# Single-precision attention and down products, deeper buffers and other due times in a fused mixture-of-experts and linear-attention kernel

## The reference

```python
x = x + 0.5 * ffn(layernorm(x))            # called A here
x = x + attn(layernorm(x))
x = x + 0.5 * ffn(layernorm(x))            # called B here

# ffn: for each token t
shared = (silu(x @ ws_gate.T) * (x @ ws_up.T)) @ ws_down.T
w, idx = top_k(sigmoid(x @ gate_weight.T), 2);  w = 2.5 * w / w.sum()
y[e]   = (silu(x @ w_gate[e].T) * (x @ w_up[e].T)) @ w_down[e].T
out    = shared + sum over the two chosen e of w_e * y[e]

# attn: xx is x shifted by one token
k, v, r = ((x * mix_i + xx * (1 - mix_i)) @ W_i.T for i in "kvr")
state_t = k_t * v_t + exp(time_decay) * state_(t-1)
o_t     = r_t * (time_first * k_t * v_t + state_t)
out     = (layernorm(o) * ln_g + ln_b) @ Wo.T
```

## Time and profile before

| | us |
|---|---|
| time, median of 3 runs | 1225.51 |
| lowest, highest | 1225.27, 1230.39 |
| the profiled execution's own time | 1227.27 |
| its span, first to last instruction | 1225.1 |
| TensorE busy | 939.6 |
| VectorE busy | 877.5 |
| GpSimd busy | 718.4 |
| ScalarE busy | 491.9 |
| mean granted TensorE clock, share of full speed | 0.921 |

### The profile page before, as it was taken

How to read it: one execution, slowest core, us unless ns; L and a number is a source line. 1 busy time by engine, 2 the same in 40 slices (tenths; PEclk the granted TensorE clock), 3 DMA queues, 4 the chain that set the end, 5 groups by cost and what they waited for, 6 DMA issues and landing times.

```text
span 1225.1 us, 26134 instructions
## 1 busy us (share of the span) xinstructions
PE 939.6 (77%) x8624; PEld 665.5 (54%) x8624; DVE 877.5 (72%) x2582; ACT 491.9 (40%) x880; POOL 718.4 (59%) x684
## 2 busy tenths in 40 slices
PE   1787878896778899879799877986799878766350
PEld 0465565673445657656675465855577544763340
DVE  5975748787978985766799887665798978626332
ACT  5433433643434544524554253432356333431130
POOL 2865666237885745477747884337843877306725
PEclk9988989998898999999899999997989988998695
DMA  9878998436275347899773499778973437775793
GB/s 297 221 157 171 251 196 192 87 92 148 83 154 116 104 106 171 193 184 192 191 161 104 134 205 201 177 190 172 210 158 109 112 108 174 167 171 175 166 256 103
DMA packets 340513, 200.86 MB, mean 164 GB/s; under 512 B 255904, under 2 KB 322592, under 8 KB 340256
## 3 DMA queue, kind: packets, MB, share of 16 engines
q1 hardware_dynamic: 314944, 131.94, 46.4%
q0 software_dynamic: 24576, 67.14, 22.7%
q10 hardware_dynamic: 864, 0.12, 0.1%
HBM read 47.05 MB, written 93.32 MB: 115 GB/s over the span
## 4 chain that ended last, share of the span: by engine, by line
POOL 30%; issue 27%; DVE 11%; PE 10%; DMA 9%; SPq 8%; ACT 3%; POOLq 0%; ACTq 0%; DVEq 0%
POOL y_got L811 11%; POOL xsB L793 7%; SPq L718 5%; POOL xsA L793 5%; DVE acc L1262 2%; DMA y_got<-ysA,y_pos 2%; POOL rstd L767 2%; POOL p_exp L784 2%; DMA ysB<-y_sb 2%; DMA y_got<-ysB,y_pos 2%; SPq L691 2%; DVE stat L1277 1%; PE ps L881 1%; POOL acc L819 1%; PE ps L883 1%
## 5 line engine op out<-in xcount | busy, mean ns | idle before, releaser
L881 PE MATMUL ps<-xq,w_hi 128*128 128x128 f16 x1280 | 236.7, 228 | 82.3 <-DMA xq<-xsB 49.3
L883 PE MATMUL ps<-xq,w_hi 128*128 128x128 f16 x1280 | 236.4, 228 | 0.0
L885 PE MATMUL ps<-xq,w_lo 128*128 128x128 f16 x1280 | 236.1, 228 | 0.0
L1262 DVE SCALAR_TENSOR_TENSOR acc<-y_got,share,acc 128x256 f32<-128x256 f32 x256 | 125.1, 530 | 127.0 <-DMA y_got<-ysB,y_pos 78.0
L905 PE MATMUL ps<-wd_hi,hid_h 128*128 (+1 forms) x576 | 161.1, 280 | 51.9 <-issue 20.4
L881 PEld LDWEIGHTS ps<-xq,w_hi 128*128 x1280 | 131.7, 103 | 96.4 <-DMA xq<-xsB 53.3
L793 POOL DMA_INDIRECT xsB<-rows,pos x128 | 135.1, 1056 | 70.2 <-issue 37.2
L793 POOL DMA_INDIRECT xsA<-rows,pos x128 | 135.8, 1061 | 67.1 <-issue 37.4
L1111 ACT CAST hid_h<-hid 128x512 f16<-128x512 f32 x144 | 89.0, 618 | 211.1 <-DVE hid L1234 196.4
L811 POOL DMA_INDIRECT y_got<-ysB,y_pos x128 | 130.2, 1017 | 62.5 <-issue 38.8
L907 PE MATMUL ps<-wd_hi,hid_l 128*128 (+1 forms) x576 | 161.4, 280 | 0.0
(11 more groups left out here) (157 smaller groups left out, 2148.0 us busy)
## 6 DMA issues: line engine op xcount, KB each, us to landing
ysA<-y_sb SPq DMA_DIRECT2D x40, 512.0 KB, 3.5
ysB<-y_sb SPq DMA_DIRECT2D x40, 512.0 KB, 3.6
acc<-in_x_dram SPq DMA_DIRECT2D x16, 512.0 KB, 4.9
out_dram<-acc SPq DMA_DIRECT2D x16, 512.0 KB
xsA<-zeros SPq DMA_DIRECT2D x36, 128.0 KB
xsB<-zeros SPq DMA_DIRECT2D x36, 128.0 KB
acc<-in_w_chunks_dram SPq DMA_DIRECT2D x10, 384.0 KB, 8.8
xq<-xsA SPq DMA_TRANSPOSE x160
```

The source lines that it names most:

```text
L881: nc.tensor.matmul(half, w_hi[2 * k + b][:, cols], hi, start=(j == 0 and k == 0), stop=False, skip_group_check=True)
L883: nc.tensor.matmul(half, w_hi[2 * k + b][:, cols], lo, start=False, stop=False, skip_group_check=True)
L885: mm = nc.tensor.matmul(half, w_lo[2 * k + b][:, cols], hi, start=False, stop=(j == 3 and k == KC - 1), skip_group_check=True)
L1262: ins = v.scalar_tensor_tensor(out=acc[:, s, j, :], in0=y_got[:, j, k, :], scalar=share[:, s, j, k:k + 1], in1=acc[:, s, j, :], op0=ALU.mu ...
```

## The change

- **Down products**: `wd` holds the unscaled weights in single precision, and each of a chunk's four products is one matmul on `hid` in single precision. `hidden_hi` and `hidden_lo` are gone, and the scale of 256 from `resid` and `weights`.
- **Attention**: `a32` and `ao32` hold single-precision weights. ScalarE's `part` writes the scaled rows of k, v and r (three copies each half), VectorE's `mix` adds the shifted rows (two instructions for each of the three), and `k_proj`, `v_proj`, `r_proj` multiply them: 12 matmuls of 512 columns a sequence. The turned rows are no longer split, o is not split, `r_copy` is gone (`receive` reads PSUM, one instruction for each half), and `out_proj` has 8 matmuls. `part` of a sequence waits until all projections of the sequence before are over; `scan` waits for `scan_turn` and `out_proj` of the sequence before; `k_sb` is a buffer of its own.
- **Start**: two DMAs for each chunk of weights instead of one; down and attention weights are not split.
- **Buffers**: `xq` 4 for 3, `y_sb` 3 for 2, `hid` 4 for 2; `carry` and `pos32` have two halves, by the group's number, so that only the group before the last must be through.
- **Groups and order**: A has 3, 4, 5, 4 sequences. Constants of the due times are other ones, each kind of task, sequence and group has an offset of its own, and the planner's rules on `table`, `gate_up` and `top2` are stricter.

```diff
-SIZES = {"A": (2, 4, 5, 5), "B": (5, 5, 4, 2)}
+SIZES = {'A': (3, 4, 5, 4), 'B': (5, 5, 4, 2)}
-N_ROWS, N_XT, N_XQ, N_Y, N_HID, N_XC = 3, 2, 3, 2, 2, 2
+N_ROWS, N_XT, N_XQ, N_Y, N_HID = 3, 2, 4, 3, 4
-    PACE = 36.0
-    FIRST_A = 16.6
-    FIRST_T = 104.7
-    A_LEAD = 247.1
-    A_GAP = 32.8
-    E_LEAD = 40.2
-    B_LAG = 82.0
-    EB_LAG = 5.0
-    E_GAP = 6.3
-    EB_GAP = 4.5
-    G_LAG = 135.3
+    PACE = 32
+    FIRST_A = 8.5
+    FIRST_T = 101.8
+    A_LEAD = 246.4
+    A_GAP = 26.1
+    E_LEAD = 33.4
+    B_LAG = 72.6
+    EB_LAG = 65.5
+    E_GAP = 6.4
+    EB_GAP = 8.8
+    G_LAG = 100.3
...
-                    nc.tensor.matmul(half, hid_h[:, b, tok], w_hi[DOWN][:, :, cols], start=(first and j % 2 == 0),
-                                     stop=False, skip_group_check=True)
-                    nc.tensor.matmul(half, hid_l[:, b, tok], w_hi[DOWN][:, :, cols], start=False, stop=False,
-                                     skip_group_check=True)
-                    mm = nc.tensor.matmul(half, hid_h[:, b, tok], w_lo[DOWN][:, :, cols], start=False,
+                    mm = nc.tensor.matmul(half, hid[:, b, tok], wd[:, :, cols], start=(first and j % 2 == 0),
                                           stop=(last and j % 2 == 1), skip_group_check=True)
...
+            def project(w, s, m):
+                if (s, m) == (0, 0):
+                    pe.wait_ge(attn_in, 16)
+                bank = bank_free(f"{w}_proj", (s, m), 0)
+                pe.wait_ge(mix_done, val("mix", s, w, per=KC))
+                for k in range(KC):
+                    mm = nc.tensor.matmul(ps[:, bank, :], a32[:, "kvr".index(w), k, m * P:(m + 1) * P],
+                                          mixed[w][:, k, :], start=(k == 0), stop=(k == KC - 1))
+                mm.then_inc(proj_done[w], 1)
...
+                for w, mix in (("k", MIX_K), ("v", MIX_V), ("r", MIX_R)):
+                    ins = nc.scalar.activation(mixed[w][:, m, :], ps[:, bank_of("turn2", (s,), m), :], ACT.Copy,
+                                               scale=chan[:, mix, m:m + 1])
+                ins.then_inc(parted, 1)
...
+                for m in range(KC):
+                    v.scalar_tensor_tensor(out=mixed[w][:, m, 1:T], in0=ps[:, bank_of("turn2", (s,), m), 0:T - 1],
+                                           scalar=less_mix[:, "kvr".index(w), m:m + 1], in1=mixed[w][:, m, 1:T],
+                                           op0=ALU.mult, op1=ALU.add).then_inc(mix_done, 1)
```

More of the change, by code:

```diff
@@ L131, in run @@
         events = [(at, None) for at in {0.0, *self.not_before.values()}]
-        now, pair = 0.0, None
+        now, pair, quads, table = 0.0, None, 0, None
         while events:
@@ L169, in run @@
                         continue
+                    if k[0] == "table" and table and not all(
+                            (name, table) in over for name in ("y_places", "table_turn", "tails")):
+                        continue
+                    if k[0] == "gate_up" and k[1][0] == "E" and turn["quads"][k[1][1:]] != quads:
+                        continue
                     if best is None or self.urgency[k] < self.urgency[best]:
@@ L337, in schedule @@
[L337 to L343, removed]
@@ L439, in follows @@
             return "chunks", None, key
-        if name in ("silu", "gated", "hidden_hi", "hidden_lo", "down"):
+        if name in ("silu", "gated", "down"):
             return "chunks", key
@@ L511, in program @@
         norm2 = kv_sb.rearrange("p m t -> p (m t)").rearrange("p (j c) -> p j c", j=NT)
-        b_wide = r_sb[:, 0, 0:KC * P].rearrange("p (k n) -> p k n", k=KC)
-        xc_h = sb("xc_h", [P, N_XC, KC, T], F16)
-        xc_l = sb("xc_l", [P, N_XC, KC, T], F16)
-        oh = sb("oh", [P, KC, T], F16)
-        ol = sb("ol", [P, KC, T], F16)
+        b_wide = mixed["r"][:, 0, 0:KC * P].rearrange("p (k n) -> p k n", k=KC)
         o_bias = sb("o_bias", [P, C])
@@ L524, in program @@
         hid = sb("hid", [P, N_HID, T])
-        hid_h = sb("hid_h", [P, N_HID, T], F16)
-        hid_l = sb("hid_l", [P, N_HID, T], F16)
         ident = sb("ident", [P, P])
@@ L658, in released, with both @@
             return (bias_out, 1) if name == "o_bias" else (centered, 1)
+        def both(name, s, **more):
+            return max(val(name, s, m, **more) for m in range(KC))
         def uses(n, buf, of):
@@ L891, in down @@
                 i = chunk_no[key]
-                pe.wait_ge(hi_done, i + 1)
-                pe.wait_ge(lo_done, i + 1)
+                pe.wait_ge(gated_done, i + 1)
+                if what == "S" and i < 2 * NSH:
+                    pe.wait_ge(wd_in[0], 16 * NSH)
+                if what == "E" and which[1] == 0:
+                    for part in (1, 2):
+                        pe.wait_ge(wd_in[part], 16 * (SPLITS[part][1] - SPLITS[part][0]))
                 first = what == "E" or which[1] == 0
@@ L951, in total @@
                 pe.wait_ge(carry_done, val("choose", f, last))
-                nc.tensor.matmul(ps[:, bank, 0:NE], ones[:], carry[f][:, (last + 1) % 2, :], start=True, stop=True)\
+                nc.tensor.matmul(ps[:, bank, 0:NE], ones[:], carry[f][:, g % 2, (last + 1) % 2, :], start=True, stop=True)\
                     .then_inc(total_done, 1)
@@ L968, in turn2 @@
                     mm.then_inc(turned2, 1)
-            def project(s, bank, which, m):
-                cols, n = slice(m * P, (m + 1) * P), s % N_XC
-                for part, to, tok in ((0, ps[:, bank, :], slice(0, T)), (1, ps[:, bank, 1:T], slice(0, T - 1))):
-                    w = 2 * which + part
-                    for k in range(KC):
-                        hi, lo = xc_h[:, n, k, tok], xc_l[:, n, k, tok]
-                        nc.tensor.matmul(to, a_hi[:, w, k, cols], hi, start=(part == 0 and k == 0), stop=False,
-                                         skip_group_check=True)
-                        nc.tensor.matmul(to, a_hi[:, w, k, cols], lo, start=False, stop=False, skip_group_check=True)
-                        mm = nc.tensor.matmul(to, a_lo[:, w, k, cols], hi, start=False,
-                                              stop=(part == 1 and k == KC - 1), skip_group_check=True)
-                return mm
```

405 lines of the change are left out of this document (150 added, 255 removed).

## The result

The changed kernel takes 1145.17 us (1141.22 to 1148.64), against 1225.43 beside it: ratio 0.9335, 95% interval 0.9294 to 0.9376. The forecast was 1165, with 1105 to 1235 as its range. The profiled execution took 1141.22 us, with a span of 1139.2.

A forecast was written before the change was run, and what follows sets the result against it. It took a mixed bound: no engine full, TensorE, VectorE and GpSimd near 85% in attention. Terms: 1225.1 + 20 - 14 - 27 - 8 - 5 - 25 = 1166, stated as 1165 us, range 1105 to 1235.

The forecast's parts named there:

- TensorE's price: Single-precision matmuls at 0.43 us (256 columns) and 0.86 us (512): TensorE +29 us net, +20 on the path.
- The way over the occupancy: Second estimate of the whole time: TensorE's 969 us at 88% occupancy, plus 62 us at both ends, gives 1163 us.
- VectorE's and ScalarE's cuts: Removed splits and copies, less the added mixing: busy time net some -127 us on VectorE, -125 on ScalarE.
- The chunk's chain: Expert chunks lose a cast, a subtraction and two handovers before the down product: -14 us (0 to -28).
- The bursts: Attention bursts, some 540 us in all, gain 5% from VectorE's cut: -27 us.
- GpSimd: Fewer conflicts with two-input VectorE instructions might return 18 us of GpSimd time, up to 10 us overall; left out of the sum.
- The queues: Fetched quads get four xq buffers for three, which shortens TensorE's waits: -8 us (0 to -20).
- The start: Ahead of the first quads, weights come in twice as many transfers and less is split: -5 us (0 to -10).
- The order at the end: Last rows and routing go before group B's quads, which fill TensorE's 25.05 us gap: -25 us (0 to -45).
- The order elsewhere: Earlier routing by halved carry and pos32, and three sequences first in group A: together 0, between -20 and +20 us.
- The rival of the closed gaps: The order closes TensorE's gaps throughout, so TensorE reaches 93%: 1104 us, chance 0.2.
- TensorE takes all of it: Between 27 and 1190 us TensorE's occupancy stays at 81%: 1258 us, slower; decides under 83.3%; chance 0.13.

The follow-up runs named there:

- e1: Changed kernel's operations and buffers with the old kernel's due times and group sizes, no offsets, planned again: 1206.03 us, ratio 0.9861.
- e3: Changed kernel with its new due-time constants but all offsets at zero, planned again: 1204.56 us, ratio 0.9857.
- e10: Changed kernel with every due-time offset rounded to a whole microsecond, planned again: 1220.75 us, ratio 0.9977.
- e7: Changed kernel in its own order, without the matmuls of the rows' low half in routed quads (71 us of TensorE): 1130.36 us, ratio 0.9219.
- e6: As e5, but each chunk's down product also waits for the added subtraction: 1161.16 us, ratio 0.9475.
- e2: Old kernel's operations and buffers with the new due times, offsets, group sizes and stricter planner rules: 1293.68 us, ratio 1.059.
- e5: Changed kernel in its own order, with one unused VectorE subtraction added behind each chunk's gating: 1161.34 us, ratio 0.9484.
- e8: Changed kernel in its own order, with GpSimd's output bias additions replaced by short ones: 1130.37 us, ratio 0.9244.
- e11: Changed kernel and due times with the old three xq, two y and two hid buffers, planned again: 1227.78 us, ratio 1.0022.
- e12: Changed kernel with group B's quads due 20 us, not 65.5 us, after their group's last rows, planned again: 1223.0 us, ratio 1.0005.

## Why the prediction was right, and where it was not

*TensorE's price* was right in every unit: 0.43 and 0.86 us. Busy time rose by 14 and not by 29 us. e1 and e3, with the same matmuls, have 969.6 and 974.4 us busy at mean clocks of 0.924 and 0.923; the changed kernel has 954.0 at 0.950. So the 29 us are there, and in the denser order some 15 are back, with a higher granted clock. The way over the occupancy hit: 954.0 us from 27.4 to 1100 us is 88.9%, for 88% forecast. That it was 88% was a choice, and that it came out is luck: in e10 the same measure, with 62 us for both ends, is 85%. The +20 us on the path were too many: at e7's price, 15 us for 71, 29 us cost 6.

*VectorE's and ScalarE's cuts*, -123 and -114 for -127 and -125, were right. *The chunk's chain*, -14, didn't come: the down product waits longer than before on VectorE and ScalarE (37.0 for 27.9 us), and in e6 the longer chain costs nothing in this order.

*The bursts*, -27: they are 62 us shorter, but this doesn't show the mechanism. e2 has none of VectorE's cut and bursts as short, 402 us, and in e1 36 us of the bursts' 58 come back in the pauses. What bears on the mechanism is VectorE's price in a fixed order (e5: 16 us for 93), by which the cut of 123 is worth 21 us, near the -27. The 540 us that the term was taken from are too many: from the first to the last bias of each group it is 465. In the third group the biases came from 44 to 37 us apart on average, with one step of 83.

*GpSimd.* The 512 indirect DMAs take 512.3 us for 531.8, 19.5 less, with the same instructions. The Trainium skill (Advanced Engine Details and Errata, GPSIMD Details) has a conflict of GpSimd with VectorE instructions of two SBUF inputs, and the estimate was 18 us. e5 and e8 agree with it in both directions: 102 us of such an instruction added to VectorE stretch GpSimd by 13 us, and 37 us of GpSimd's addition removed shorten VectorE's other work by 16. Two things hold the agreement in bounds. Of e5's 13 us only 8.1 are in the indirect DMAs (520.4 for 512.3), so 102.9 us of hid_l explain less than half of the 19.5. And of e8's 16 us some 6 are in `var_eps`, an instruction with one input (307 to 182 ns each), which two inputs don't cover. The sum did without this; at e8's price GpSimd's 31 us are worth 9 to 12, and it belonged in it.

*The queues*, -8: TensorE's wait for quads fell by 35.5 us, 25 of it the gap. What the fourth xq buffer did is open (e11). *The start*, -5: the first bias comes 9 us later, with three sequences in the first group and not two; in e1, with two, it comes 8 us earlier.

*The order at the end*, -25: that the later due time of B's quads closes the gap is shown by e12, and before and e1 against all others agree. The forecast effect on the time is not there: the gap went and the tail is 6 us longer, with 27 us more of TensorE's work in it and the DMA engines full from 1000 to 1100 us.

*The order elsewhere*, 0 between -20 and +20, is the term that failed. With the changed operations, e3 and e1 against the changed kernel put it at 60 us, e10 at 75. My range for it was too small because I read due times as an intention, one by one, and not as the seed of one list order out of many. TensorE's own account shows the two steps. The span is its busy and its idle time: 939.6 + 285.5 us before, 969.6 + 237.2 in e1, 954.0 + 185.2 in the changed kernel. Operations and buffers under the old due times bring 48 us less idle time for 30 us more work; the particular order brings 52 us less idle time and 16 us less busy time.

How the 80 us divide between operations and order is not settled by this. Against the kernel before, with the order it came with, the new operations in four other plans bring between 17 us and nothing (e1, e3, e10, e12). But the old operations in another plan lose as much: e2 is 72 us slower than the kernel before, and 88 us slower than e1. It may be that both kernels have an order fitted to them and that the operations are worth most of the 80 us. No run takes the old plan to a near neighbour, as e10 does with the new one. An estimate from the prices in the fixed order lies between: VectorE's 123 us at 0.17 and GpSimd's 31 at 0.4, less TensorE's 29 at 0.21, are some 27 us; it leaves out what shorter chains, more buffers and the "issue" waits do.

The sum came near by luck in good part. Its terms for the order were too small, those for the chain, the queues, the tail and the start too large, and 42 us of "issue" waits and 21 of waits for the state, which went, had no term.

*The rival of the closed gaps*, 1104, is 41 us from the result, the forecast's 1165 is 20. Its condition was TensorE at 93%; measured are 88.9%, and the pauses still last 309 us. *TensorE takes all of it* didn't come. The neighbouring plans at 1220 to 1230 us (e10, e11) have its time but not its occupancy: by the prediction's measure, with 62 us for both ends, TensorE is at 85 and 84% in them, above the 83.3% at which it was to decide.

What stays open: how much of the 80 us the order brings and how much the operations; what the single-precision down products are worth against the split ones under an equally good order; what ended the "issue" waits; and which of e10's turned choices costs the most.

## What to carry to other kernels

When an order comes from a greedy planner, an edit and its new plan are one change: run neighbours of the plan (rounded parameters, offsets at zero) before giving the edit the credit, since here such runs of the new kernel lie 60 to 80 us above it, some as far up as the kernel before. And do the same to the old kernel's plan, or a fitted plan is compared with unfitted ones; that was left out here. Prices of an engine's time are read from runs in which the order is kept and one engine's work is added or removed; even then the other engines' work can stretch or shrink with it, and the busy share doesn't give them. And near the end look at what stands ahead of the last producers in each queue: in e12 non-urgent gathers and stores ahead of scatters and fetches left TensorE idle for 45 us.

## What the runs showed of the hardware

With less to do in the same order TensorE was granted a lower clock: without 71 us of matmuls its busy time fell by only 45 us (mean clock 0.950 to 0.917, e7), and the same matmuls in a denser order are busy for 954.0 us at 0.950 where they took 969.6 at 0.924 (e1). VectorE and GpSimd stretch each other's instructions, by 13 us for 102 us added on one side (e5) and by 16 us for 37 on the other (e8). Single-precision matmuls of 256 columns come every 0.43 us although their two weight loads are 0.195 us each, and those of 512 every 0.86 us, twice as far apart with the same loads, so these lie beside the matmuls.
